# An attention-and-experts kernel: prologue, convolution stage and shared down projection rearranged

## The chip, the cores and the metric

The kernel runs on one core of a Trainium2 chip. The metric is device time in microseconds (us), the median of several executions. Engines are named as the profile names them: PE is TensorE (matmuls), DVE is VectorE, ACT is ScalarE, POOL is GpSimd, SP is SyncE, which here only issues transfers.

## The reference

`x` and `ctx_2048` are (8, 256, 512). Two blocks follow one another. Cut to what matters:

```python
# block 1: long convolution as attention, v = layernorm(x), x1 = x2 = ctx
kv  = v[:, h, :, None, :] * x2[:, h, None, :, :]        # 32 heads h of 8 rows: outer product over rows
y   = irfft(rfft(kv) * rfft(k[h]))[..., :L] + kv * bias  # causal convolution over L = 512
x   = x + einsum('bhijl,bhil->bhjl', y, x1)
# block 2: experts on layernorm(x)
scores = sigmoid(xf @ gate_w.T); top 2 of 8, weights normalised, times 2.5
shared = (silu(xf @ shared_wg.T) * (xf @ shared_wu.T)) @ shared_wd.T      # 704 hidden
routed = sum over the 2 picked experts of w * expert(xf)                  # 352 hidden each
x = x + shared + routed
```

## The kernel before, in words

The convolution is done as matmuls against Toeplitz blocks of the filter. Every f32 operand is split into a high and a low f16 part, and a product is three matmuls (high·high, high·low, low·high: `split_products`, lines 753 to 755). A head has 4 output blocks and 10 block pairs, so 30 matmuls of 128x512.

The 32 heads run in order, in four groups `g` of `HG` = 8. For head `s`, GpSimd makes the outer product `kv` (`outer`, L603, four instructions), ScalarE rounds it to the high part (`high_parts`, L1013) and reverses the filter (`turn_filter`, L1006), and the low part is a subtraction, on VectorE (`low_parts`, L1247) if `s` is in `DVE_LOWS` and on GpSimd (L628, four instructions) otherwise. TensorE convolves (`convolve`), VectorE multiplies each bank with the context (`products`, L1261) and sums (`total`, L1268). The buffers are a ring: `kv` has two, the parts have three, banks 0 to 3 hold a convolution, banks 4 and 5 the shared experts' gate and up, and banks 6 and 7 are taken in turn by all small work (`take`, `turn_bank`), in an order written out in `turn_order`: who takes a bank waits until the one two places before has been read.

Around the heads, in each engine's program by hand: before group `g` its rows are normalised (`value_moments`, `inverse_root`, `values`), transposed by TensorE (`prepare`, L775) and copied out (`turned`, L1045). The skip term takes `skip_product` (L1299), a matmul (`skip_sum`, L789) and `skip_term` (L1306, L1307) for each of four tiles. After the group the result is transposed back (`mix_out`) and added (`mixed`, L1415), its moments taken (`moments`, L1274), `feed_norm` and `feed_low` write its two parts, DMA transposes them (`turn_rows`), and while group `g` is convolved the rows of `g-1` go through `logits`, `scores`, `pick`, `ranks`, `pairs` (the row numbers in the experts' table), `gate_up` (six steps), `gated`, and one group later `down` and `add_shared`. The 704 hidden units are five tiles of 128 and one half tile of 64, which is tile 0. When the last group is done the experts' weights have been loaded (`expert`), and 39 tiles of 128 routed rows are computed in a loop to the end.

The prologue: SyncE loads the filters, the first rows `x_tok`, the constants and `ctx_hidden` (`cT`), in this order. The filters are split and stored to be read back repeated for every partition. The first rows are normalised as one piece, transposed through banks 6 and 7, copied by VectorE (`first_turned`, L1234), multiplied by GpSimd (`first_outer`, L619), rounded by ScalarE (L1018), and subtracted by VectorE (`first_low_parts`, L1241).

Of the kernel before, what the change touches and what calls it, by code (L numbers as in the profile page):

```python
# [50 lines left out]
DVE_LOWS = (0, 1, 5) + tuple(range(HG, H, 2))  # L51
# [3 lines left out]
def xattn_moe(nc, x, ctx, ctx_hidden, skip, krev, gate_w, shared_w, expert_w, consts, table0, zeros, out):  # L55
    split_filters = nc.dram_tensor("split_filters", [H, 2 * KREV], F16).ap()
    filters = bass.AP(split_filters.tensor, 0, [[2 * KREV, H], [1, P], [KREV, 2], [1, L]])
    x_rows = x.rearrange("b (g r) l -> g b r l", r=RG)
# [5 lines left out]
    with ExitStack() as stack:  # L64
# [138 lines left out]
        const_in = sem("const_in")  # L203
        small_in = sem("small_in")
        x_in = [sem(f"x_in{g}") for g in range(G)]
        ctx_in = [sem(f"ctx_in{g}") for g in range(G)]
        cT_in = [sem(f"cT_in{g}") for g in range(G)]
        filt_all_in = sem("filt_all_in")
# [103 lines left out]
        def turn_bank(name, g, k):  # L312

            n = sum(len(list(turns_of(*w))) for w in turn_order[:turn_order.index((name, g))])
            return bank[6 + (n + k) % 2]

# [29 lines left out]
        def shared_loads(i):  # L346

            return 2 if 0 < i < DOWN_AT else 1
# [37 lines left out]
        def _(sp):  # L386
            def load_filter(s):
                if s > 0:
                    sp.wait_ge(filt_ready, s)
# [19 lines left out]
            def load_shared(i):  # L409
                if i >= DOWN_AT:  # L410
# [35 lines left out]
            sp.dma_start(gate_raw[:], gate_w).then_inc(small_in, 16)  # L446
            sp.wait_ge(filt_stored, 16)
            load_filter(0)
            load_rows(ctx_tok, ctx_rows[0], ctx_in[0])
# [25 lines left out]
            for g in range(1, G):  # L475
# [12 lines left out]
                if g < G - 1:  # L488
# [8 lines left out]
                for h in range(5, HG + 2):  # L497
                    if s0 + h < H:
                        load_filter(s0 + h)

# [91 lines left out]
        def _(pool):  # L592
# [15 lines left out]
            def first_outer():  # L608

                v, c = heads(vT[0])[:, :, 0:NH], heads(cT[0])[:, :, 0:NH]  # L610
                pool.wait_ge(cT_in[0], 16)
                for q in range(Q):
                    pool.wait_ge(tokT_done, q + 1)
                    pairs_of = B // Q
                    to = by_tile(kv[0], q).rearrange("p a (b j i) -> p a b j i", i=NH, j=NH)
# [1057 lines left out]
```

## Time and profile before

| | us |
|---|---|
| median of 3 runs (758.6 to 763.07) | 761.96 |
| the profiled execution | 757.6 |
| its span | 755.8 |

The profile cuts the span in 40 slices and gives for each engine the tenths of busy time:

```profile
PE   2786976969989979999999998979899999999991
...
DVE  4799599767877668776778576784422221212210
...
POOL 2889988484783663874677404740132323223231
PEclk9999898979999998999999998989999999999996
```

PEclk is the TensorE clock that was granted, in tenths. A slice is 18.9 us: the heads end in slice 24, the rest is the experts. Idle time before a group of instructions is put down to what ended last.

### The profile page before, as it was taken

How to read it: one execution, taken by the hardware profiler on the slowest of the kernel's cores; microseconds unless marked ns; L12 is line 12 of the kernel's file. 1: busy time of each engine (PE TensorE's matmuls, PEld its weight loads, DVE VectorE, ACT ScalarE, POOL GpSimd, SP SyncE). 2: the span in 40 equal slices, each digit the busy share in tenths (PEclk: the TensorE clock that was granted, in tenths of full speed). 3: DMA queues.
4: the chain of work that ended last, by engine and by line, in shares of the span. 5: the costliest groups of instructions: out<-in, count | busy, mean ns of one | idle time of the engine just before them, and what ended most of it. 6: DMA issues, size and time to landing. Idle time of an engine off the chain costs nothing.

```text
span 755.8 us, 11521 instructions
## 1 busy us (share of the span) xinstructions
PE 663.5 (88%) x3441; PEld 329.3 (44%) x3442; DVE 438.5 (58%) x702; ACT 292.9 (39%) x362; POOL 387.2 (51%) x333
## 2 busy tenths in 40 slices
PE   2786976969989979999999998979899999999991
PEld 1332432434444434443444443425455555555550
DVE  4799599767877668776778576784422221212210
ACT  4336646534223443323243049543423232232320
POOL 2889988484783663874677404740132323223231
PEclk9999898979999998999999998989999999999996
DMA  7933222701333800313305079878897887878743
GB/s 204 275 97 97 84 69 68 162 9 29 126 79 74 183 15 19 113 38 70 84 15 200 14 270 262 297 195 262 162 125 127 138 128 129 131 125 140 129 62 42
DMA packets 130964, 91.56 MB, mean 121 GB/s; under 512 B 97664, under 2 KB 111488, under 8 KB 130368
## 3 DMA queue, kind: packets, MB, share of 16 engines
q1 hardware_dynamic: 121728, 72.44, 38.9%
q0 software_dynamic: 9200, 18.65, 14.0%
q8 instruction: 21, 0.34, 0.2%
q14 instruction: 15, 0.12, 0.1%
HBM read 44.35 MB, written 25.68 MB: 93 GB/s over the span
## 4 chain that ended last, share of the span: by engine, by line
PE 61%; DVE 14%; ACT 8%; POOL 7%; DMA 4%; issue 4%; SPq 1%; POOLq 0%; DVEq 0%; ACTq 0%
PE banks L753 20%; PE banks L754 19%; PE banks L755 19%; POOL arena L603 4%; PE banks L775 2%; DVE stats L1274 2%; DMA arena<-split_filters 2%; POOL arena L628 2%; DVE mixT L1268 1%; DVE arena L1261 1%; DMA out<-xf,ids 1%; ACT arena L1092 1%; DVE arena L1247 1%; DVE hm L1395 1%; DVE arena L1429 1%
## 5 line engine op out<-in xcount | busy, mean ns | idle before, releaser
L603 POOL TENSOR_TENSOR arena<-arena 128x512 f32<-128x512 f32 x124 | 136.1, 1130 | 67.0 <-DVE arena L1247 65.7
L716 POOL DMA_INDIRECT out<-xf,ids x39 | 61.2, 1569 | 185.8 <-DMA out<-xf,ids 142.5
L753 PE MATMUL banks<-arena 128*128 128x512 f16 x320 | 124.6, 389 | 21.0 <-DVE arena L1261 11.1
L754 PE MATMUL banks<-arena 128*128 128x512 f16 x320 | 124.2, 388 | 0.8 <-issue 0.8
L755 PE MATMUL banks<-arena 128*128 128x512 f16 x320 | 124.0, 387 | 0.0
L1261 DVE TENSOR_TENSOR arena<-banks,arena 128x512 f32<-128x512 f32 x128 | 81.3, 682 | 33.8 <-PE banks L755 28.6
L753 PE MATMUL banks<-arena,normed 128*128 x312 | 97.5, 313 | 0.9 <-DVE hm L1570 0.9
L754 PE MATMUL banks<-arena,normed 128*128 x312 | 97.5, 313 | 0.0
L755 PE MATMUL banks<-arena,normed 128*128 x312 | 97.5, 313 | 0.0
L1013 ACT ACTIVATE arena<-arena 128x2048 f16<-128x2048 f32 x31 | 59.1, 1906 | 87.5 <-POOL arena L603 87.5
L1568 DVE SCALAR_TENSOR_TENSOR hm<-banks,silu 128x256 f32<-128x256 f32 x39 | 16.5, 424 | 130.8 <-PE banks L755 120.0
L628 POOL TENSOR_TENSOR arena<-arena 128x512 f16<-128x512 f32 x68 | 78.8, 1193 | 7.6 <-ACT arena L1013 7.5
L1268 DVE TENSOR_REDUCE mixT<-arena 128x256 f32<-128x2048 f32 x32 | 73.1, 2285 | 1.0
L753 PE MATMUL banks<-xf,arena 128*128 128x512 f16 x176 | 69.2, 393 | 2.9 <-DVE hm L1395 2.8
L754 PE MATMUL banks<-xf,arena 128*128 128x512 f16 x176 | 69.0, 392 | 0.0
L755 PE MATMUL banks<-xf,arena 128*128 128x512 f16 x176 | 68.8, 391 | 0.0
L1006 ACT ACTIVATE arena<-arena 128x1024 f16<-128x1024 f16 x32 | 33.7, 1054 | 84.4 <-PE banks L755 71.3
L753 PEld LDWEIGHTS banks<-arena 128*128 128x128 f16 x320 | 31.9, 100 | 63.1 <-issue 20.4
L755 PEld LDWEIGHTS banks<-arena 128*128 128x128 f16 x320 | 31.9, 100 | 40.4 <-issue 4.4
L754 PEld LDWEIGHTS banks<-arena 128*128 128x128 f16 x320 | 31.9, 100 | 38.9 <-issue 4.8
L753 PE MATMUL banks<-arena,mixT 128*128 x117 | 44.4, 379 | 4.4 <-issue 2.7
L1185 ACT CAST x_tok<-hm 128x384 f16<-128x384 f32 x37 | 18.9, 511 | 73.5 <-DVE hm L1570 71.5
(168 smaller groups left out, 1095.6 us busy)
## 6 DMA issues: line engine op xcount, KB each, us to landing
arena<-split_filters SPq DMA_DIRECT2D x32, 256.0 KB
arena<-in_expert_w SPq DMA_DIRECT2D x12, 544.0 KB, 8.8
stages<-in_expert_w SPq DMA_DIRECT2D x10, 544.0 KB, 5.9
arena<-in_ctx_hidden SPq DMA_DIRECT2D x4, 1024.0 KB, 8.1
arena<-in_ctx SPq DMA_DIRECT2D x8, 512.0 KB, 6.5
x_tok<-in_x SPq DMA_DIRECT2D x6, 512.0 KB, 7.6
out<-x_tok SPq DMA_DIRECT2D x6, 512.0 KB, 6.0
x_tok<-in_expert_w SPq DMA_DIRECT2D x5, 544.0 KB
```

Of the source, the lines that this page charges most:

```text
L603: nc.gpsimd.tensor_tensor(kv[s % 2][:, lb * COLS:(lb + 1) * COLS].rearrange("p (b j i) -> p b j i", i=NH, j=NH), v[:, a, None, :].to_broad ...
L628: nc.gpsimd.tensor_tensor(kvl[s % SPLITS][:, c], kv[s % 2][:, c], kvh[s % SPLITS][:, c], ALU.subtract).then_inc(kvl_by_pool, 1)
L716: nc.gpsimd.indirect_dma_start(out=out, out_offset=bass.IndirectOffsetOnAxis(ap=ids[slot][:, 0:1], axis=0), in_=yg[slot], in_offset=None, ...
L753: nc.tensor.matmul(dst, wh, xh, start=(k == 0), stop=False)
L754: nc.tensor.matmul(dst, wh, xl, start=False, stop=False)
L755: last = nc.tensor.matmul(dst, wl, xh, start=False, stop=(k == n - 1))
L1006: nc.scalar.activation(filt[s % 2].rearrange("p (t l) -> p t l", t=2), back, ACT.Copy).then_inc(filt_ready, 1)
L1013: nc.scalar.activation(kvh[s % SPLITS], kv[s % 2], ACT.Copy).then_inc(kvh_ready, 1)
L1185: nc.scalar.copy(by_token[slot][:, 0:FK * P], hm[:, 0:FK * P]).then_inc(r_hh, 1)
L1261: nc.vector.tensor_tensor(prod[:, n * COLS:(n + 1) * COLS].rearrange("p (b j i) -> p b j i", i=NH, j=NH), bank[n].rearrange("p (b j i) -> ...
L1268: nc.vector.tensor_reduce(heads(mixT)[:, :, h * NH:(h + 1) * NH], prod.rearrange("p (a j i) -> p a j i", i=NH, j=NH), AX_X, ALU.add).then_ ...
L1568: nc.vector.scalar_tensor_tensor(out=hm[:, 0:whole], in0=bank[1][:, 0:whole], scalar=1 / WS, in1=silu[:, 0:whole], op0=ALU.mult, op1=ALU.mult)
```

## The change

The arithmetic is the same. The parts:

1. Prologue. `cT[0]` is loaded by a transfer that ScalarE issues first of all. The first rows come as two halves with a semaphore each, the constants as three (the small columns between the halves, then the identity, then the masks). The first filter is loaded directly as f32 and split by ScalarE and VectorE, no longer through the stored copy. Moments, root and shift go by halves; the four transposed tiles go to banks 4 to 7; `first_outer` is on VectorE and reads the banks; the copies to `vT` are on ScalarE, behind its rounding.
2. `DVE_LOWS`: heads 3, 7, 9 and 11 come to VectorE; 8, 10 and 12 go to GpSimd.
3. The skip term of group 1 moves from heads 4 to 7 into heads 11 and 12. The normalising of the next rows is split over two heads on TensorE and ScalarE. `rank` is behind `prep` in the turn order, `pairs` runs at the sixth head, and `inverse_root` behind the outer product.
4. After a group: the moments of tiles 0 and 1 are taken between the additions, `down(g-2, 0)` stands between the halves of `mix_out`, `add_shared` ahead of `feed_low`, and in group 1 `products` of head 9 ahead of `feed_low`. The context of group 2 is loaded later.
5. The half tile of `down`: the low part is written to rows 64 to 127 of `hTh` and the weights are doubled there, so one matmul gives two of the three terms: two matmuls in place of three.

```diff
-DVE_LOWS = (0, 1, 5) + tuple(range(HG, H, 2))
+DVE_LOWS = (0, 1, 3, 5, 7, 9, 11) + tuple(range(2 * HG - 2, H, 2))
...
-        turn_order = [("prep", 0), ("skip", 0), ("prep", 1), ("skip", 1)]
+        turn_order = [("skip", 0), ("prep", 1)]
         for g in range(1, G):
-            turn_order += [("out", g - 1), ("feed", g - 1), ("xf", g - 1), ("rank", g - 1)]
-            turn_order += [("prep", g + 1), ("skip", g + 1)] if g < G - 1 else []
+            turn_order += [("out", g - 1), ("feed", g - 1), ("xf", g - 1)]
+            turn_order += [("skip", 1)] if g == 1 else []
+            turn_order += [("prep", g + 1)] if g < G - 1 else []
+            turn_order += [("rank", g - 1)]
+            turn_order += [("skip", g + 1)] if g < G - 1 else []
...
             sp.dma_start(filt_all, krev).then_inc(filt_all_in, 16)
-            load_rows(x_tok[0], x_rows[0], x_in[0])
-            sp.dma_start(con[:], consts).then_inc(const_in, 16)
-            load_hidden(0)
+            for half in range(2):
+                for b2 in range(2):
+                    sp.dma_start(x_tok[0][b2 * RG:(b2 + 1) * RG, 2 * half:2 * half + 2, :],
+                                 x_rows[0].rearrange("(q t) r l -> t r q l", t=2)[b2][:, 2 * half:2 * half + 2, :]
+                                 ).then_inc(first_x_in[half], 16)
+                if half == 0:
+                    sp.dma_start(con[:, 4 * P:CONST_W], consts[:, 4 * P:CONST_W]).then_inc(small_const_in, 16)
+            sp.dma_start(con[:, 0:P], consts[:, 0:P]).then_inc(const_in, 16)
+            sp.dma_start(filt_raw.bitcast(F32), first_filter).then_inc(first_filt_in, 16)
+            sp.dma_start(con[:, P:4 * P], consts[:, P:4 * P]).then_inc(masks_in, 16)
...
+            act.dma_start(cT[0], ctx_hidden[0]).then_inc(cT_in[0], 16)
             act.wait_ge(filt_all_in, 16)
...
-            values(0)
-            turn_filter(0)
+            act.wait_ge(first_shift, 1)
+            layer_norm(x_tok[0], v_ready, range(0, 2))
+            first_filter_high()
+            act.wait_ge(first_shift, 2)
+            layer_norm(x_tok[0], v_ready, range(2, Q))
             first_high_parts()
+            first_turned()
             high_parts(1)
...
+            def first_outer(q):
+                dve.wait_ge(tokT_ready, q + 1)
+                dve.wait_ge(cT_in[0], 16)
+                pairs_of = B // Q
+                v = first_bank[q].rearrange("p (a b r) -> p a b r", a=LB, b=pairs_of)[:, :, :, 0:NH]
+                c = heads(cT[0])[:, :, 0:NH]
+                to = by_tile(kv[0], q).rearrange("p a (b j i) -> p a b j i", i=NH, j=NH)
+                shape = [P, LB, NH, NH]
+                for b in range(pairs_of):
+                    a = slice(pairs_of * q + b, None, B)
+                    last = nc.vector.tensor_tensor(to[:, :, b], v[:, :, b, None, :].to_broadcast(shape),
+                                                   c[:, a, :, None].to_broadcast(shape), ALU.mult)
+                last.then_inc(first_kv, 1)
...
+            first_moments(0)
+            first_moments(1)
+            first_shift_by(0)
+            first_shift_by(1)
+            first_filter_low()
+            first_outer(0)
+            first_outer(1)
+            first_low(0)
+            first_outer(2)
+            first_low(1)
+            first_outer(3)
+            first_low(2)
+            first_low(3)
...
+            def down_products(g, q, first=0, end=SM):
+                dst, c = down_bank(g, q), slice(q * P, (q + 1) * P)
+                for k in range(first, end):
+                    w = slice(k * L, (k + 1) * L)
+                    nc.tensor.matmul(dst, hTh[:, k, c], d_h[:, w], start=(k == 0), stop=False)
+                    if half_tile(k):
+                        last = nc.tensor.matmul(dst, hTh[0:HALF, k, c], d_l[0:HALF, w], start=False, stop=False)
+                    else:
+                        nc.tensor.matmul(dst, hTl[:, k, c], d_h[:, w], start=False, stop=False)
+                        last = nc.tensor.matmul(dst, hTh[:, k, c], d_l[:, w], start=False, stop=(k == SM - 1))
+                return last
...
             for g in range(1, G):
                 s0 = g * HG
                 convolve(s0)
-                mix_out(g - 1)
+                mix_out(g - 1, range(0, 2))
                 if g > 1:
                     if g == 2:
                         pe.wait_ge(shared_l, SH_PIECES)
-                    for q in range(Q):
+                    down(g - 2, 0)
+                mix_out(g - 1, range(2, Q))
+                if g > 1:
+                    for q in range(1, Q):
                         down(g - 2, q)
...
                 convolve(s0 + 3, range(LB - 1, LB) if g == 1 else range(LB))
+                if g == 1:
+                    skip_sum(1, 0)
+                    skip_sum(1, 1)
                 gate_up(g - 1, 1)
-                ranks(g - 1)
+                if g == G - 1:
+                    ranks(g - 1)
                 convolve(s0 + 4)
+                if g == 1:
+                    skip_sum(1, 2)
+                    skip_sum(1, 3)
+                gate_up(g - 1, 2)
                 if g < G - 1:
                     prepare(g + 1, range(0, 2))
-                gate_up(g - 1, 2)
+                convolve(s0 + 5)
                 if g < G - 1:
                     prepare(g + 1, range(2, Q))
-                for h in range(5, HG):
+                gate_up(g - 1, 3)
+                if g < G - 1:
+                    ranks(g - 1)
+                for h in range(6, HG):
...
             def mixed(g):
                 for q in range(Q):
-                    if g == G - 1 and q == 2:
-                        expert(0, 1)
+                    if q == 2:
+                        if g == G - 1:
+                            expert(0, 1)
+                        dve.wait_ge(x1_done, Q * g + q)
+                        tile_moments(x_tok[g % 3], range(0, 2))
...
                 if g == 1:
+                    products(s0 + 1, 1, g)
                     feed_low(0, range(0, 2))
-                    products(s0 + 1, 1, g)
+                    total(s0 + 1, 1)
                     feed_low(0, range(2, Q))
-                    total(s0 + 1, 1)
...
+                if g == 1:
+                    skip_product(1, 0)
+                    skip_product(1, 1)
                 pick(g - 1)
...
-                    if h == 4:
+                    if h == (6 if g < G - 1 else 4):
                         pairs(g - 1)
```

## Rows read from the trace of the kernel before

**Rows 1.** The page: busy time of each engine, and the chain that ended last by engine
```profile
PE 663.5 (88%) x3441; PEld 329.3 (44%) x3442; DVE 438.5 (58%) x702; ACT 292.9 (39%) x362; POOL 387.2 (51%) x333
...
PE 61%; DVE 14%; ACT 8%; POOL 7%; DMA 4%; issue 4%; SPq 1%; POOLq 0%; DVEq 0%; ACTq 0%
```

**Rows 2.** Windows by stage: length, busy of each engine, granted clock, DMA share, GB/s
```profile
0.00:23.57 23.57, 3.84 (x17) 3.05 (x18) 10.95 (x23) 9.06 (x12) 9.07 (x16) 1.00 0.84 210
23.57:105.91 82.34, 68.43 (x273) 29.95 (x274) 70.09 (x75) 41.63 (x39) 74.78 (x62) 0.94 0.42 117
105.91:215.04 109.13, 94.06 (x465) 43.95 (x466) 88.20 (x129) 49.80 (x52) 76.54 (x68) 0.92 0.31 82
215.04:331.45 116.41, 107.73 (x538) 49.93 (x537) 84.67 (x132) 43.64 (x47) 70.47 (x66) 0.97 0.33 80
331.45:437.51 106.06, 102.26 (x514) 46.28 (x513) 72.78 (x110) 32.36 (x35) 62.96 (x59) 0.98 0.26 70
437.51:525.65 88.14, 77.24 (x395) 34.39 (x393) 63.99 (x122) 49.61 (x60) 32.18 (x25) 0.92 0.84 262
525.65:755.83 230.18, 209.89 (x1245) 121.80 (x1245) 47.81 (x116) 66.74 (x118) 61.20 (x39) 0.97 0.76 122
```

**Rows 3.** Waits of TensorE up to 530 us: total, times, longest
```profile
PE banks L775 <- ACT normed L1029: 16.5, 3, 13.8
PE banks L753 <- DVE arena L1261: 11.1, 4, 6.2
PE banks L775 <- DVE next_row L1341: 9.9, 2, 5.1
...
PE banks L775 <- ACT arena L1045: 5.8, 1, 5.8
...
PE banks L775 <- DVE x_tok L1415: 2.7, 2, 2.2
PE banks L775 <- DVE arena L1415: 2.2, 1, 2.2
```

**Rows 4.** The chain that ended last: start, length, what
```profile
2.04 6.24 DMA x_tok<-in_x
...
15.80 6.06 POOL arena L619 x8
...
29.24 0.22 PE banks L754
...
445.05 2.48 DVE stats L1274 x4
```

**Rows 5.** Windows inside the first eleven microseconds, columns as in rows 2
```profile
3.00:8.00 5.00, 0.00 (x0) 0.00 (x0) 0.81 (x1) 1.10 (x2) 0.00 (x0) 1.00 1.05 244
8.00:11.00 3.00, 0.00 (x0) 0.00 (x0) 2.66 (x7) 0.00 (x0) 0.00 (x0) 1.00 1.01 401
```

**Rows 6.** Groups of GpSimd, 23.57 to 105.91 us: count, busy, mean ns, idle before
```profile
L603 POOL TENSOR_TENSOR arena<-arena 128x512 f32<-128x512 f32 x36 | 41.4, 1181 | 5.0 <-DVE arena L1247 4.5 <-POOL arena L628 0.2
L628 POOL TENSOR_TENSOR arena<-arena 128x512 f16<-128x512 f32 x20 | 24.3, 1245 | 0.0
```

**Rows 7.** Timeline of GpSimd, 96 to 106 us
```profile
100.88 2.13 POOL L658 TENSOR_TENSOR arena<-stages,arena 128x1024 f16<-128x1024 f32 x1
```

**Rows 8.** Groups of VectorE, 23.57 to 105.91 us
```profile
L1261 DVE TENSOR_TENSOR arena<-banks,arena 128x512 f32<-128x512 f32 x30 | 19.2, 681 | 11.7 <-PE banks L755 11.7
...
L1247 DVE TENSOR_TENSOR arena<-arena 128x2048 f16<-128x2048 f32 x3 | 9.2, 3050 | 0.0
L1299 DVE SCALAR_TENSOR_TENSOR hm<-arena,skip_col,normed 128x512 f32<-128x512 f32 x4 | 7.4, 1843 | 0.0
...
L1306 DVE TENSOR_TENSOR banks<-banks,arena 128x512 f32<-128x512 f32 x8 | 5.5, 688 | 0.0
```

**Rows 9.** Windows around two stalls, columns as in rows 2
```profile
278.40:288.50 10.10, 4.50 (x15) 2.33 (x16) 6.16 (x20) 5.57 (x9) 6.72 (x6) 0.66 0.01 2
338.90:346.50 7.60, 5.41 (x21) 2.25 (x21) 6.53 (x14) 1.06 (x1) 7.50 (x8) 0.78 0.12 35
```

More of the change, by code:

```diff
@@ L315, in turn_bank, with backward @@
             return bank[6 + (n + k) % 2]
+        first_bank = bank[4:4 + Q]
+        def backward(raw, parts):
+            return bass.AP(raw.tensor, raw.offset + L - 1, [raw.ap[0], [L, parts], [-1, L]])
         def toeplitz(s, part, d):
@@ L409, in load_shared @@
             def load_shared(i):
+                if i == DOWN_AT:
+                    sp.dma_start(shared_raw(i)[:, L:SH_PIECE], shared_w[:, L:SH_PIECE]).then_inc(shared_in[i], 16)
+                    for copy in range(2):
+                        sp.dma_start(shared_raw(i)[copy * HALF:(copy + 1) * HALF, 0:L], shared_w[0:HALF, 0:L]
+                                     ).then_inc(shared_in[i], 16)
+                    return
                 if i >= DOWN_AT:
@@ L857, in _ @@
             pe.wait_ge(const_in, 16)
-            prepare(0)
+            for q in range(Q):
+                pe.wait_ge(v_ready, q + 1)
+                transpose_tile(first_bank[q], lambda lb: normed[:, q, lb * P:(lb + 1) * P], tokT_ready)
             convolve(0)
+            pe.wait_ge(tokT_done, Q)
+            pe.wait_ge(masks_in, 16)
             skip_sum(0, 0)
@@ L866, in _ @@
                 convolve(s)
-            prepare(1)
+            prepare(1, range(0, 2))
             convolve(5)
-            skip_sum(1, 0)
-            skip_sum(1, 1)
-            convolve(6)
-            skip_sum(1, 2)
-            skip_sum(1, 3)
-            convolve(7)
+            prepare(1, range(2, Q))
+            for s in range(6, HG):
+                convolve(s)
             for g in range(1, G):
@@ L1025, in next_parts, with layer_norm @@
                     high_parts(s + 1)
-            def layer_norm(src, done):
-                for q in range(Q):
+            def layer_norm(src, done, tiles=range(Q)):
+                for q in tiles:
                     nc.scalar.activation(normed[:, q, :], src[:, q, :], ACT.Identity, bias=shift[:, q:q + 1],
@@ L1270, in total, with tile_moments, moments @@
                                         ).then_inc(mix_done, 1)
-            def moments(src):
-                link(*[nc.vector.bn_stats(stats[:, q, :], src[:, q, :]) for q in range(Q)])
+            def tile_moments(src, tiles):
+                link(*[nc.vector.bn_stats(stats[:, q, :], src[:, q, :]) for q in tiles])
+            def moments(src, tiles=range(Q)):
+                tile_moments(src, tiles)
                 link(*[nc.vector.bn_aggr(meanvar[:, q, :], stats[:, q, :]) for q in range(Q)])
@@ L1417, in mixed @@
                 dve.wait_ge(x1_done, Q * (g + 1))
[L1418 removed]
+                moments(x_tok[g % 3], range(2, Q))
             def mixed_shift(g):
[L1422 removed]
+                dve.wait_ge(rstd_ready, 2 * g + 2 if g < G - 1 else 2 * G - 1)
                 shift_by(shift_ready)
```

192 lines of the change are left out of this document (107 added, 85 removed).

## The prediction, on record before the change was run

> **What bounds the kernel now.** The page comes first [rows 1]: TensorE is busy for 88% of the span and makes up 61% of the chain that ended last. It is the bound on average, so what can be gained is its idle time, its time at the lower clock, and matmuls left out. The windows by stage [rows 2] say where these lie. The first seven lines are the prologue, group 0, groups 1, 2 and 3, the shared experts' last part with the weights' arrival, and the routed tiles. TensorE is idle for 19.7 us of the prologue, 13.9 of group 0, 15.1 of group 1, 8.7 of group 2, 3.8 of group 3. The routed tiles, 230 us, are full and untouched. In group 0 GpSimd is busy 74.8 of 82.3 us and VectorE 70.1: three engines are near their limit there, and a stall mended on one meets another. In group 1 VectorE has 88.2 of 109.1; in groups 2 and 3 TensorE alone is full.
>
> The waits of TensorE [rows 3] name the stalls: the first rows' normalising (13.8 us of 16.5), products of VectorE that come late (6.2 us in group 1, most of the rest at the end of group 0), `prepare` waiting for `rank_used` (next_row, 5.1 in group 2, the rest in group 1), `prepare` waiting for ScalarE's copies (5.8, group 0), and `mix_out`, whose third tile waits for the addition of the first (2.2 in each of groups 2 and 3).
>
> **Prologue.** Before, the chain [rows 4] has the rows landing at 8.3 us and `first_outer` on GpSimd, eight instructions in 6.06 us. The transfer engines are full from 3 us on [rows 5]: 244 GB/s while rows of 2 KB and the constants pass, 401 GB/s while the context passes with its larger packets. The context, 1.05 MB, takes 2.6 us of them. Now it goes ahead of the rows or beside them. The rows' last half then lands after 80 KB of filters, 1.05 MB of rows and the context: I start at 3 us with 0.1 MB moved, add 1.03 MB / 244 = 4.2 and 2.6, and get 9.8, with the landing 10.1 us; before it was 8.3. If the context didn't delay the rows it would be 7.5. The first half doesn't help by itself: its shift stands on VectorE behind the second half's moments.
>
> The Trainium skill ("DMA: Bandwidth & Descriptors", section "Issuing engines are not separate DMA queues") says that transfers from several issuing engines interleave on the same 16 engines and save only the issuing time. No row here has a transfer that ScalarE issued. By that rule the landing is 10.1, by separate paths 7.5, and the prologue's gain 2.1 or about 4.5 us.
>
> From landing to the first outer product it was 8.3 to 15.8, 7.5 us [rows 4]. Of these go half the moments (1.2 of 2.48 for four tiles [rows 4]), the root of the first half, about 1.1 as it now lies beside the second half's moments, and the copy before the product, 0.7 (a bank of 512, as L1261 [rows 8]). So VectorE starts at 10.1 + 4.5 = 14.6, or a little before that with the filter, and sets the pace. Its filter part, eight products of 256 elements and four quarter subtractions aren't in the trace in this form. A product is at least half of 0.68 [rows 8] and at most GpSimd's 6.06 / 8 = 0.76 [rows 4]; I take 0.4, since the form is L1261's. A quarter of a low part is 3.05 / 4 = 0.76 [rows 8]. With the filter's 0.7 that is 0.7 + 3.1 + 3.1 = 6.9, and the first convolution starts at 21.5, not 23.57 [rows 2]. The copies to `vT` now stand behind the rounding on ScalarE, so I put head 1's outer product at 22.9, 1 us later than before (15.80 + 6.06 [rows 4]); its chain, with 4 x 1.18 [rows 6] and a low part of up to 3.05 [rows 8] in it, ends about when TensorE is done with head 0 and two skip matmuls. If it doesn't, the gain at head 1 is nothing. I let head 1 start 2.1 earlier. Gain 2.1, bounds 0 (products at 0.76) and 4.5.
>
> **Group 0.** GpSimd's sum decides. It ends outer product 9 and the shared piece behind it at 103.0 [rows 7]. Two low parts leave it: eight instructions by 1.245 = 10.0 us [rows 6]. With the earlier start (I take 1.4 of the 2.1, because outer 5 still waits for VectorE's low part of head 3) that is 91.6. Low part 8 is now its own: 4.6, ending at 96.2, and head 8's last block, 12 matmuls of 0.217 [rows 4], ends at 98.8; before, head 8 ended at 105.9 + 30 x 0.217 = 112.4. VectorE gains two low parts (6.1) and loses group 1's skip term (4 products of 1.84 or less, 8 additions of 0.69 [rows 8], about 12), so it ends nearly when GpSimd does. I take off 1.2 for six outer products whose pieces may be slower than the mean of 1.18 [rows 6] while VectorE runs low parts beside them. Head 8 ends 12.5 us earlier, 10.4 of them group 0's. The 5.8 us wait is gone with it, since ScalarE's copies are asked for before `kv` runs out.
>
> **Group 1.** The wait for `next_row` (4.8 of the 9.9 [rows 3]) goes, and `products` of head 9 come 3 us sooner. But the skip term arrives: VectorE has 88.2 + 12 = 100, and waits some 5 us for ScalarE inside `gated`. That makes 105 of a stage that took 109.1. TensorE would need 94.1 + 3.4 for the skip matmuls, less what it loses at half clock (0.92 over 109.1 us is 17 us at half; I put the work in them at 9, so 4.6). So VectorE is the bound and the stage can't give more than about 4. And TensorE's program is in order: `skip_sum(1, 0)` and `(1, 2)` stand ahead of `gate_up`, while their products are queued behind `gated` and the moments. I expect three new waits of 3 to 5 us, at head 11 and twice at `skip_sum`. Gain 2.0, bounds -6 and 8.
>
> **Group 2.** 8.7 us of idle [rows 2] go, 2.2 of them `mix_out` and 5.1 `prepare` [rows 3], and with them the half clock behind it: 0.66 over 10.1 us [rows 9] is 6.8 us at half, of which TensorE worked 3.9 (from the end of the wait on), so 1.95. Four matmuls fewer give 0.9. Sum 11.5; I take 10.5, since `skip_sum` may wait as in group 1. VectorE has 84.7 of 116.4, cover enough for the new places of `pairs` and the moments.
>
> **Group 3.** 2.2 for `mix_out`; 0.78 over 7.6 us [rows 9] is 3.3 at half, 1.7 lost; 0.9 of matmuls. Sum 4.8, taken 4.6.
>
> **Tail.** Behind group 3 the chain goes through the moments of four tiles, 2.48 at 445.05 [rows 4]. Two are now taken while VectorE waits for the transposes: 0.9. `down(2, 0)` is 0.2 shorter on the same chain and `down(3)` 0.9. Gain 2.0. The weights are asked for when buffers come free, so they move along.
>
> **Sum.** 2.1 + 10.4 + 2.0 + 10.5 + 4.6 + 2.0 = 31.6 us. Against the profiled execution's own 757.6 that is 726.0. The median of the runs lies 4.4 above that execution and the lowest 1.0, so I put a median 2 above: 728.
>
> **Rivals.** (a) Group 1 gives everything back: VectorE is the bound there and in group 0's end, the new waits at `skip_sum` reach 6 us each and cost the clock as well. Group 1 loses 6, group 0 gives 8 only, and the prologue nothing: 728 + 8 + 2.4 + 2.1 = 740. For it speaks the row of group 1 [rows 2]; against it that half of TensorE's old waits there are named and removed. (b) TensorE's stalls close better than I walk through them: prologue 4.5, group 1 gives 8, group 2 all of its 11.5: 2.4 + 6 + 1 more than the sum, 718. (c) Slower. The clock stays at its lower level. Group 1 has a mean of 0.92 [rows 2], 17 us at half. If the waits of 3 to 5 us that follow each other from head 8 to 12 kept the clock low through that stretch, some 50 us of matmuls would run at half and cost 50: 728 + 50 = 778. It decides from 32 us of matmuls more at half upward. Against it: in group 0, with 13.9 us of idle, the mean is 0.94 and 10 us were at half [rows 2], not the whole stage. The Trainium skill ("TensorE: Matmul & The Clock Gate", section "What's actually happening") has the throttled state as the default, which activity lifts; by it more waits are more such stretches. (d) No change to speak of: the routed part doesn't start earlier, since weights or the table of rows set its start. Then 757. Against it: TensorE is busy 77 of 88 us in that stage, and the transfers there wait for kernel events.
>
> **Chances.** Forecast (720 to 736) 0.54, (a) 0.22, (b) 0.17, (c) 0.04, (d) 0.03. All but (c) and (d) are faster: 0.93, 0.03 within 0.5%, 0.04 slower. Half a per cent, 3.8 us, is what runs that spread over 4.5 us can tell. The range, 716 to 743, leaves out about the outer half of (b) and (c), (d) and a little of (a).
>
> **What would show it.** Prologue: `x_tok` landing near 10 us and the first convolution near 21.5; near 19 is the other price. Group 0: head 8 ends near 99 and GpSimd has no gap in it. Group 1: waits of L789 or L753 for L1299 and L1261, VectorE over 95% busy, head 16 starting near 201. Group 2: no wait for L1341 or L1415, clock 1.00, length 105 to 106. Group 3: 101.5. Three matmuls in four tiles' worth of `down` are two. I am wrong if head 8 isn't earlier by 10, if the waits at `skip_sum` reach 6 us, or if the granted clock falls below 0.9 in a stage.

## The result, and the profile after

The changed kernel takes 754.39 us (median of 9 runs, 750.37 to 758.23), the kernel before 758.93 (9 runs, 757.66 to 763.07) beside it: a ratio of 0.993, 95% interval 0.990 to 0.996. It is faster by 0.7%, about 4.5 us, where 31.6 were forecast; 754 lies outside the range of 716 to 743. Measured again later it was 752.3 against 759.7, 0.9905 (0.988 to 0.993).

The page of the changed kernel, the lines that answer to [rows 1]:

```profile
PE 662.5 (88%) x3425; PEld 327.5 (44%) x3426; DVE 438.8 (58%) x710; ACT 293.9 (39%) x366; POOL 390.2 (52%) x322
...
PE 34%; DVE 20%; POOL 18%; ACT 10%; DMA 7%; issue 7%; another core or an unknown queue 2%; SPq 1%; POOLq 0%; DVEq 0%; ACTq 0%
```

TensorE is as busy as before, but its part of the chain that ended last fell from 61% to 34%, and GpSimd's rose from 7% to 18%. The kernel has not lost its waits: they have changed their owner. The windows by stage, cut at the same events as [rows 2]:

```profile
0.00:21.36 21.36, 3.81 (x17) 3.18 (x19) 10.53 (x28) 9.49 (x15) 1.63 (x7) 1.00 0.89 219
21.36:94.64 73.28, 62.30 (x265) 27.34 (x265) 62.54 (x70) 40.78 (x41) 71.43 (x56) 0.98 0.49 135
94.64:207.19 112.55, 101.17 (x473) 45.30 (x474) 89.01 (x133) 49.78 (x53) 84.44 (x69) 0.92 0.30 78
207.19:324.62 117.43, 108.24 (x535) 49.28 (x534) 89.01 (x132) 43.52 (x48) 72.14 (x66) 0.97 0.35 81
324.62:432.51 107.89, 101.42 (x511) 46.13 (x509) 75.41 (x114) 34.16 (x36) 66.73 (x61) 0.98 0.28 68
432.51:519.26 86.75, 74.05 (x386) 33.97 (x385) 64.50 (x122) 49.48 (x60) 32.18 (x25) 0.96 0.83 254
519.26:752.60 233.34, 211.47 (x1245) 122.28 (x1245) 47.82 (x116) 66.65 (x118) 61.66 (x39) 0.96 0.79 126
```

Groups 2 and 3 (lines 4 and 5) are longer in this trace than before, 117.4 for 116.4 and 107.9 for 106.1, though two waits were taken out of the one and one out of the other. The change is ahead by 2.2 us at the first convolution, 7.0 at head 8's end, 7.9 at head 16, 6.8 at head 24, 5.0 at the end of the heads, and 3.2 at the end. (A second pair of traces, below, divides the gain otherwise among the stages.) TensorE's waits up to 530 us, for [rows 3]:

```profile
PE banks L799 <- ACT normed L1087: 14.0, 1, 14.0
PE banks L777 <- DVE hm L1504: 13.5, 4, 4.6
PE banks L777 <- issue: 8.7, 3, 3.7
PE banks L777 <- DVE arena L1366: 8.4, 8, 3.0
PE banks L813 <- DVE hm L1408: 5.7, 5, 3.1
PE banks L777 <- DMA mixT<-x_tok: 4.2, 1, 4.2
```

The waits for `next_row` (L1341), for ScalarE's copies (L1045) and for `mix_out`'s addition (L1415) are gone, as forecast. In their place stand 13.5 us for `hm`, the gated product that `gate_up` needs to reuse its bank, 5.7 at `skip_sum` (L813), and 4.2 for the first routed tile's transposed rows. None of the three is among [rows 3]. In the kernel before, the same view has 3.4 us for `hm` in four waits (longest 1.4) and 0.5 at `skip_sum`, and the first routed tile waited 2.7.

### The profile page after: what moved, and what is told of

Same layout as the page of the kernel before. It is cut to its first block, busy times and chain, and to the rows that moved or that the text cites. A ratio compares the mean times of both kernels' runs of the same rounds, so it can differ in the third digit from the quotient of the medians.

```text
span 752.6 us, 11505 instructions
## 1 busy us (share of the span) xinstructions
PE 662.5 (88%) x3425; PEld 327.5 (44%) x3426; DVE 438.8 (58%) x710; ACT 293.9 (39%) x366; POOL 390.2 (52%) x322
## 4 chain that ended last, share of the span: by engine, by line
PE 34%; DVE 20%; POOL 18%; ACT 10%; DMA 7%; issue 7%; another core or an unknown queue 2%; SPq 1%; POOLq 0%; DVEq 0%; ACTq 0%
PE banks L777 11%; PE banks L778 11%; PE banks L779 11%; POOL arena L635 9%; POOL arena L650 4%; DMA x_tok<-in_x 3%; DVE arena L1366 2%; DVE mixT L1373 2%; POOL pair_table L674 2%; DVE arena L1542 2%; POOL arena L680 2%; DVE hm L1504 2%; DVE stats L1379 1%; ACT arena L1149 1%
## 5 line engine op out<-in xcount | busy, mean ns | idle before, releaser
L635 POOL TENSOR_TENSOR arena<-arena 128x512 f32<-128x512 f32 x124 | 142.0, 1177 | 74.3 <-ACT arena L1102 36.8
L777 PE MATMUL banks<-arena 128*128 128x512 f16 x320 | 125.2, 391 | 21.4 <-DVE arena L1366 8.4
L778 PE MATMUL banks<-arena,normed 128*128 x312 | 97.7, 313 | 0.0
L779 PE MATMUL banks<-arena,normed 128*128 x312 | 97.7, 313 | 0.0
L1366 DVE TENSOR_TENSOR arena<-banks,arena 128x512 f32<-128x512 f32 x128 | 81.0, 683 | 25.1 <-PE banks L779 21.2
L777 PE MATMUL banks<-xf,arena 128*128 128x512 f16 x176 | 69.0, 392 | 13.5 <-DVE hm L1504 13.5
```

The source lines that it names most:

```text
L635: nc.gpsimd.tensor_tensor(kv[s % 2][:, lb * COLS:(lb + 1) * COLS].rearrange("p (b j i) -> p b j i", i=NH, j=NH), v[:, a, None, :].to_broad ...
L777: nc.tensor.matmul(dst, wh, xh, start=(k == 0), stop=False)
L778: nc.tensor.matmul(dst, wh, xl, start=False, stop=False)
L779: last = nc.tensor.matmul(dst, wl, xh, start=False, stop=(k == n - 1))
L1366: nc.vector.tensor_tensor(prod[:, n * COLS:(n + 1) * COLS].rearrange("p (b j i) -> p b j i", i=NH, j=NH), bank[n].rearrange("p (b j i) -> ...
```

## The experiments

The kernel before measured 759.1, 753.4, 759.7 and 761.5 in the four series, so ratios are to the kernel before of the same series, and milestones are read from the traces. First four, one edit each on the changed kernel.

**The moments of group 3's rows.** In group 2 VectorE stood before `gated` in a wait for rows that landed late. The chain there, changed kernel:

```profile
236.60 6.51 DMA out<-x_tok
...
243.78 12.27 DMA x_tok<-in_x
...
256.08 2.48 DVE stats L1379 x4
...
259.20 0.70 DVE hm L1504
```

The edit puts the moments back behind `pick`:

```diff
-                if 1 < g < G - 1:
-                    value_moments(g + 1)
                 gated(g - 1, 0)
...
-                    if h == 3 and g == 1:
+                    if h == 3 and g < G - 1:
                         value_moments(g + 1)
```

> The changed kernel with one edit undone: in group 2 the moments of the next rows are taken again behind gated and pick, not ahead of them. Theory A: the 5.4 us that VectorE waits for the rows' transfer stand in front of hm, TensorE waits 4.6 us for it and loses 2.6 more at the lower clock. Without it group 2 is 5 to 8 us shorter and the kernel 5 to 8 us faster than the changed one, near 748. Theory B: GpSimd's chain is late there too, the wait only changes its name: under 2 us.

753.07 us, 0.9911 (0.989 to 0.994). Head 20 starts at 265.8, not 268.2, but head 21 at 282.5 and head 24 at 324.6, both as before the edit. The first wait for `hm` in group 2 is 3.4 for 4.6 us: the moments were late, and what stands behind them nearly as late. Theory B.

**Low part 8.** It was given back to VectorE, with low parts 9 and 11 to GpSimd:

```diff
-DVE_LOWS = (0, 1, 3, 5, 7, 9, 11) + tuple(range(2 * HG - 2, H, 2))
+DVE_LOWS = (0, 1, 3, 5, 7) + tuple(range(HG, H, 2))
```

> The changed kernel with the low parts of heads 8, 10 and 12 on VectorE and 9, 11 on GpSimd, as before the change; heads 3 and 7 stay with VectorE. Theory A: head 8 waits for GpSimd (6.5 us for its low part in place of 4.5), so head 8 ends 3 to 5 us earlier than 105.5; what is left at head 16 is smaller, since VectorE is the limit in group 1. Theory B: GpSimd's speed, slowed by VectorE beside it, is the limit whoever has head 8: head 8 ends within 1 us of 105.5.

751.42, 0.9907 (0.988 to 0.993). Head 8 ends at 98.8, 6.8 earlier. That is the time the prediction gave before it took off 1.2, though it had GpSimd do this low part. Theory A, by more than it said. Yet head 10 starts at 115.5 (changed kernel 115.1), and head 16 at 206.7 (207.2). TensorE waits 6.2 us at `skip_sum(1, 0)` rather than 3.1. Group 1 takes up what group 0 gives here.

**The sending of pairs**, eight indirect transfers on GpSimd:

```diff
                     elif h == 0 and g >= 2:
-                        send_pairs()
                     elif g > 0 and h == 1:
                         inverse_root(2 * g)
+                        if g >= 2:
+                            send_pairs()
```

> The changed kernel with the eight indirect transfers of send_pairs moved on GpSimd from ahead of the second head's low part to behind its inverse root, where it idles 11 us. Theory A: in groups 2 and 3 TensorE's gains were eaten because those 10 us stand ahead of the outer product, the rounding and feed_norm: groups 2 and 3 get 2 to 4 us shorter each, with the wait for hm in group 3 (3.4 us) mostly gone. Theory B: feed_norm is late for VectorE's sake: no change beyond 1 us.

748.89, 0.9877 (0.986 to 0.990). Group 2 takes 114.3, not 117.4, and group 3 up to the end of its heads 101.2, not 102.9: Theory A by the lengths. The wait for `hm` in group 3 did not mostly go, though: it is 2.6 for 3.4. The heads end 4.5 us earlier in the trace, and the end 5.8. Against the first measurement of the changed kernel (0.993) this is clear of the noise, against its second (0.9905) only just not.

**The context from SyncE's queue**, behind the rows, not from ScalarE's at the start:

```diff
+            load_hidden(0)
...
-            act.dma_start(cT[0], ctx_hidden[0]).then_inc(cT_in[0], 16)
```

> The changed kernel with the first context loaded by SyncE behind the rows, as before the change, instead of by ScalarE first of all. Theory A: both share the transfer engines, so the rows land earlier (last half near 8.5 to 9 instead of 11.2 us), and the first convolution starts 1.5 to 2.5 us earlier. Theory B: the first product then waits for the context, which lands later, and the start is no earlier than 21.4.

753.9, 0.993 (0.991 to 0.995). The first convolution starts at 21.25, not 21.36. The chain's first long piece in the changed kernel:

```profile
4.03 7.16 DMA x_tok<-in_x
```

and with the context behind the rows:

```profile
5.71 8.64 DMA arena<-in_krev
```

The rows' last half now comes earlier (VectorE's second shift at 11.1, not 13.8 us), so the context did delay them by 2.7. But the first filter, which now stands behind the context in SyncE's queue, lands at 14.4 and holds the same start. Theory B by the time, with the filter in the context's place. The prediction's price of 10.1 for the landing (11.2 measured) was the right one of its two. The Trainium skill ("DMA: Bandwidth & Descriptors", section "Issuing engines are not separate DMA queues") says that transfers started by different engines interleave on the same 16 DMA engines; the 2.7 us of this run agree.

**Three edits at once**: low parts, moments and sending.

> The changed kernel with three edits at once: low parts 9 and 11 back on GpSimd, the moments of group 3's rows back behind the picking of experts, and the sending of pairs behind GpSimd's inverse root. Theory A, the stalls are separate: head 8 ends at 98.8, group 1 takes the gain back until head 16 (206.6), groups 2 and 3 keep 3 and 2 us of the later sending (heads' end 422), and what the moments give at head 20 (2 us) is kept, since GpSimd's chain no longer waits behind the transfers: 746 to 748. Theory B, the moments only move the wait: as with the later sending alone, 748.5 to 749.5.

745.13, 0.988 (0.984 to 0.993), and 745.0 in the next series, 0.981 (0.976 to 0.987). Theory A, and a little beyond its 746 to 748: the heads end at 420, not 422. It is the best full kernel here, 1.2 to 1.9% faster than the kernel before.

**The kernel before with only the sending moved.**

```diff
                     elif h == 0 and g >= 2:
-                        send_pairs()
                     elif g > 0 and h == 1:
                         inverse_root(2 * g)
+                        if g >= 2:
+                            send_pairs()
```

> The kernel before with only the sending of pairs (8 indirect transfers, about 10 us of GpSimd) put behind its inverse root in groups 2 and 3. Theory A: in the kernel before, the late chain GpSimd, ScalarE, VectorE is hidden under TensorE's own waits for next_row and mix_out, so the edit gives less than 1.5 us: 757.5 to 760, against 5 us in the changed kernel. Theory B: the late chain costs both kernels alike: 754 to 755, and then the changed order uncovered nothing.

753.72 against 753.4: 0.9996 (0.997 to 1.003), Theory A by the time. The trace said otherwise: group 3 took 96.7 us up to the end of its heads, not 101.1. So it was run again:

> The kernel before with only the sending of pairs behind the inverse root, measured again with more rounds. In its first trace the two waits for mix_out's addition (2.2 us each) shrank to 0.5 and group 3 took 96.7 us, not 101, yet the ratio was 0.9996. Theory A, the gain is real and the first measurement missed it in its spread: ratio 0.993 to 0.996. Theory B, the gain is given back in the tail or by the clock: ratio 0.998 to 1.001, with 2 us or more lost behind the heads' end.

754.23 against 761.5: 0.992 (0.989 to 0.995), and group 3 took 98.4 with TensorE's granted clock at 1.00. My Theory A of the first run, that the sending was hidden in the kernel before, does not hold there. The two intervals don't overlap. But the edited kernel took 754 us both times: it is the kernel before that moved, 753.4 in the one series and 761.5 in the other, and there is no trace of it from either. So the size stays between nothing and 1% by the times. By the traces the heads end at 425.9 and 429.7, where the two traces of the kernel before have 432.5 and 435.5. The waits for `mix_out`'s addition, which the change removed by a new order of TensorE's program, shrink from 2.2 to 0.5 us by this one move.

**Group 1 with less VectorE work**, on the three edits. Most of group 1's skip term is left out: only an eighth of `skip_product`'s columns is computed, and `skip_term` has no multiplication. This kernel's output lacks that term.

```diff
+                w = slice(0, L // 8 if g == 1 else L)
...
+                if g != 1:
                     link(nc.vector.tensor_tensor(t, t, ctx_tok[:, q, :], ALU.mult))
```

> The kernel with the three edits, with most of VectorE's share of group 1's skip term left out (an eighth of each product's columns, and the multiplication of skip_term not done for group 1; the output lacks it): about 4 x 1.5 and 4 x 0.7 = 9 us less VectorE work in group 1. Theory A, VectorE is group 1's bound: head 16 starts 6 to 9 us earlier than with the three edits alone, and the waits at skip_sum fall below 1 us. Theory B, the waits there are of order, not of load (GpSimd's or ScalarE's chain is next): head 16 is at most 3 us earlier.

740.79. VectorE's work from head 8's end to head 16 fell by 4.5 us (85.3 to 80.7), half of what was expected. Head 16 starts at 205.3, for 206.5 and 205.7 in the two traces with the full term, and the wait at `skip_sum(1, 0)` is still 5.6, for 7.0 and 6.1. Theory B: it isn't VectorE's load. Of the 5.3 us by which the end is earlier in the trace, 3.8 lie behind the heads, where nothing was changed; the second trace with the full term has 2.9 of them too. The timeline of VectorE and ScalarE at that wait, three edits:

```profile
131.68 1.91 ACT L1060 ACTIVATE arena<-arena 128x2048 f16<-128x2048 f32 x1 [2.49 <-POOL arena L635]
133.61 1.28 ACT L1122 ACT_TABLE_LOAD   x1
134.90 0.20 ACT L1122 ACTIVATE score<-banks 128x32 f32<-128x32 f32 x1
135.12 1.28 ACT L1128 ACT_TABLE_LOAD   x1
136.41 0.59 ACT L1128 ACTIVATE silu<-banks 64x512 f32<-64x512 f32 x1
```

```profile
137.04 0.69 DVE L1504 SCALAR_TENSOR_TENSOR hm<-banks,silu 64x512 f32<-64x512 f32 x1 [6.56 <-ACT silu L1128]
138.41 0.69 DVE L1509 TENSOR_TENSOR hTh<-hm,hTh 64x512 f16<-64x512 f32 x1 [0.68 <-ACT hTh L1134]
139.13 0.75 DVE L1408 SCALAR_TENSOR_TENSOR hm<-arena,skip_col,normed 128x512 f32<-128x512 f32 x1
```

Read backwards: `skip_sum` waits for a product of VectorE (L1408), which stands behind `gated`. That waited 6.56 us for the silu. The silu stood on ScalarE behind two table loads and a high part, and the high part waited for GpSimd's outer product. VectorE is 79% busy in this stage, in the changed kernel too (89.0 of 112.6), where the prediction looked for over 95%, and it is idle at the wait.

**Work put into that wait.** On the three edits, three blocks of head 12 (18 matmuls, 3.9 us) ahead of `skip_sum(1, 0)`:

```diff
                 if g == 1:
+                    convolve(s0 + 4, range(0, LB - 1))
                     skip_sum(1, 0)
                     skip_sum(1, 1)
```

> The kernel with the three edits, with the first three blocks of head 12 (18 matmuls, 3.9 us) put ahead of skip_sum(1, 0) on TensorE, where it waits 7.0 us for VectorE's product behind gated. Theory A, the place of skip_sum is what costs group 1: head 13 starts 3 to 4 us earlier and head 16 keeps it (203), the end by as much. Theory B, the chain over GpSimd's outer product, ScalarE's high part and silu sets group 1's pace: TensorE waits for kv at head 13 or 14 instead, and head 16 is at most 1.5 us earlier.

745.08, beside 745.0 for its base in the same series. The first wait shrinks from 6.1 to 2.4 us, and one of 5.5 us opens at `skip_sum(1, 2)`, not at `kv` as Theory B said; head 13 starts at 164.7 (163.7), head 16 at 206.8 (205.7). Otherwise Theory B: group 1's pace does not come from the place of this TensorE work, and the chain over GpSimd, ScalarE and VectorE is what the timelines show at the wait.

Its base, and the two kernels themselves, were profiled again beside it.

> The kernel with the three edits once more, as the base for the next run: ratio 0.984 to 0.993, head 16 at 206.5, heads' end at 420.

> The changed kernel profiled once more. Ratio to the kernel before 0.990 to 0.996 as in the first measurement; waits of 2.6 to 4.6 us before the second products of group 1 and 2 and at the silu of group 3 at the same places.

> The kernel before, profiled once more on the chip of this series. Theory A, chips differ in their clock and transfers: its stages are each shorter or longer than in the first profile by up to 3 us in sum, with the same waits at the same places (next_row 5.1, mix_out 2.2). Theory B, the waits themselves vary from one execution to the next: the waits for mix_out's addition come and go, and a stage difference of 2 us between two kernels proves little.

The base came out as expected. The changed kernel had a span of 753.5, with its waits for `hm` and at `skip_sum` up to the heads' end the same within 0.8 us. The kernel before took 760.3 in one run, span 758.5, with the waits of [rows 3] at their places within 1.1. Its head 8 ended 2.7 us later. So single stages move by up to 3 us between executions, and a stage difference of 1 us proves nothing by itself.

The pair of second traces changes the account by stage. The change is ahead by 2.3 us at the first convolution, 8.5 at head 8's end, 7.7 at head 16, 10.8 at head 24, 9.5 at the end of the heads and 5.0 at the end. Group 2 is 3.2 us shorter there (118.9 to 115.7), not 1.0 longer, and the part behind the heads is 4.4 longer, not 1.8.

**GpSimd's outer product beside VectorE's low part.** In groups 2 and 3 of the changed kernel GpSimd needs 6.2 us for the outer product ahead of the silu. The edit, on the three, takes the low part from beside it:

```diff
-                low_parts(s0 + 4)
+                if g == 1:
+                    low_parts(s0 + 4)
...
                 gated(g - 1, 0)
+                if g > 1:
+                    low_parts(s0 + 4)
```

> The kernel with the three edits (745.1), with VectorE's low part of head s0 + 4 behind gated(g - 1, 0) in groups 2 and 3, where VectorE waits some 6 us for the silu. Theory A, the low part beside it is what makes GpSimd's outer product take 6.2 us rather than 4.1: that outer product takes 4.2, the high part and the silu come 2 us earlier, the waits for hm in groups 2 and 3 (2.8 and 2.5) fall below 1, and the end is 3 to 5 us earlier. Theory B, the low part slows the next piece of GpSimd's just as much, or picking and the moments come late instead: within 1 us of 745.

749.46, 0.986 (0.984 to 0.988), no faster than its base (0.981 and 0.988). Its timeline of GpSimd and then of VectorE in group 2:

```profile
242.67 4.14 POOL L635 TENSOR_TENSOR arena<-arena 128x512 f32<-128x512 f32 x4
258.09 4.13 POOL L635 TENSOR_TENSOR arena<-arena 128x512 f32<-128x512 f32 x4 [11.28 <-DVE arena L1352]
```

```profile
255.72 2.29 DVE L1352 TENSOR_TENSOR arena<-arena 128x2048 f16<-128x2048 f32 x1
...
259.22 2.03 DVE L1435 TENSOR_TENSOR onehot<-con,topf 128x32 f32<-128x32 f32 x2
261.28 0.99 DVE L1438 TENSOR_TENSOR picked<-onehot 128x32 f16<-128x32 f32 x1
```

Theory A holds for the mechanism: 4.14 us, and the wait for `hm` falls from 2.8 to 1.9 in group 2 and from 2.5 to 0.5 in group 3. It fails for the time: GpSimd waits 11.3 us for the late low part before its next outer product, the collision moves to the picking of experts (2.03 and 0.99 us, for 0.42 and 0.19 elsewhere), and TensorE waits 6.4 us at head 20.

**The low parts shared out as before**, on the changed kernel: `DVE_LOWS = (0, 1, 5) + tuple(range(HG, H, 2))`.

> The changed kernel with the low parts shared out as in the kernel before (VectorE 0, 1, 5 and every second from 8 on; two more for GpSimd in group 0). Theory A, GpSimd's sum sets group 0 and its gain is kept: head 8 ends at 108 to 110 and head 16 starts 3 us later than in the changed kernel (210), the end at 757. Theory B, group 1's waits at skip_sum take up any lateness of group 0, as they took up the 6.8 us of the low part of head 8: head 16 within 1.5 us of 207.2 and the end within 2 us of the changed kernel.

755.76, 0.993 (0.991 to 0.996). Head 8 ends at 104.5, 1.1 *earlier* than in the changed kernel, and head 16 starts at 210.9, 3.7 later. By head 16 and the end this is Theory A; the lateness was not taken up. Head 8 is no test of GpSimd's load here, because its own low part went to VectorE in the same edit. The run with low part 8 on VectorE differs from this one in heads 3 and 7 alone. Against it the two low parts more on GpSimd make head 8 end 5.7 us later (104.5 for 98.8) and head 16 start 4.2 later (210.9 for 206.7). The two low parts are 10 us of GpSimd by the prediction's sum. They come out as 5.7 at head 8, since without them TensorE goes from head 7 to head 8 with no wait and is the limit itself. And group 1 passes on most of a lateness that comes from GpSimd.

**The tail.** On the three edits, the last expert's weights are asked for behind the first tile's transposed rows:

```diff
                 turn_hidden(t, t % 2)
                 if t == 0:
+                    load_expert(E - 1)
```

> The kernel with the three edits, with the last expert's weights asked for behind the first routed tile's transposing transfer, not ahead of it. Theory A, the first hidden tile waits for a full set of transfer engines: its transfer takes 3 us rather than 7.5, the wait of 4.2 us at the first down product goes, and the end comes 2 to 4 us earlier. Theory B, what the first tile gains is lost at the next ones or at the weights' rounding: within 1 us.

747.84, 0.992 (0.989 to 0.995), beside 745.13. The first tile's second product starts 14.7 us behind its first, not 18.0, and then TensorE waits 3.95 us for the same kind of transfer at 521.6. Theory A is out for the time. The intervals overlap, so that the kernel is slower by 2.7 us isn't shown. That the weights take the transfer engines from one tile or from the next fits the two waits; no run shows it by itself.

## Why the prediction was wrong

Of its three signs of being wrong one came: head 8 is earlier by 7.0 us, not by 10. The waits at `skip_sum` stayed at 3.1 and below, and the lowest granted clock of a stage was 0.92.

**Prologue, 2.1: right, in part by luck.** 2.2 measured, and the first convolution at 21.4, for 21.5. But the landing was at 11.2 rather than 10.1, and VectorE started at 15.1, not 14.6. Its filter part, products and subtractions then took 6.1 us, not 6.9, and the two misses cancel.

**Group 0, 10.4: half of it came.** Head 8 ended 7.0 earlier, not 12.5, at 105.5. The step "Two low parts leave it: eight instructions by 1.245" held. (GpSimd gets to low part 8 at 93.4, for 91.6.) The next, low part 8 "is now its own: 4.6, ending at 96.2", is mis-sized. The timeline of GpSimd, changed kernel:

```profile
93.38 6.54 POOL L650 TENSOR_TENSOR arena<-arena 128x512 f16<-128x512 f32 x4
```

It took 6.54 and ended at 99.9. One of its four pieces alone took 3.21 us, from 94.5 to 97.7, while VectorE's low part of the next head ran beside it. TensorE stood before head 8 for 3.7 us, and from 97.8 on did 27 of its 30 matmuls at a mean granted clock of 0.78 (98.0 to 105.6 us). So the last block began at 102.8 and not as soon as the low part was done: about 3 us of the lateness lie there, and the prediction had no term for them. I had a row for the cause: VectorE's three low parts took 3.05 us each in group 0 [rows 8], where the run with the low part behind `gated` has one at 2.29. Both engines are slowed when they meet, and I allowed 1.2 us for it in six outer products and nothing in the low part.

**Group 1, 2.0: 0.85 came, inside the bounds, and the reason was wrong.** "VectorE has 88.2 + 12 = 100" became 89.0 of 112.6 us. From head 8's end to head 16 VectorE's work went from 82.4 to 85.0, not up by 12: there is one low part less in the stretch, and `skip_product` takes 1.3 us rather than the 1.84 of [rows 8]. "So VectorE is the bound" fell with the run that took its work away. A wait of 3.1 at `skip_sum` came as forecast, but from the chain described above. The runs with low part 8 on VectorE and with head 12 ahead of `skip_sum` show that group 1 swallows time brought to TensorE there. The run with the low parts of before shows that it does not swallow a later GpSimd.

**Group 2, 10.5: the step that failed.** The stage is 1.0 us longer in the first pair of traces and 3.2 shorter in the second. The step subtracted TensorE's waits and the half clock behind them, with "VectorE has 84.7 of 116.4, cover enough". The waits did go, and others came: TensorE waited 8.7 us in group 2 before, and now waits 9.2, of them 6.2 for `hm` and 1.9 at `skip_sum`, with the stage's granted clock at 0.97 both times. A busy share is no cover. The question was how soon the next thing would be needed. In group 3, where moments play no part, both traces show it. ScalarE before:

```profile
376.34 1.91 ACT L1013 ACTIVATE arena<-arena 128x2048 f16<-128x2048 f32 x1 [1.78 <-POOL arena L603]
378.27 1.28 ACT L1065 ACT_TABLE_LOAD   x1
379.57 0.20 ACT L1065 ACTIVATE score<-banks 128x32 f32<-128x32 f32 x1
379.78 1.28 ACT L1071 ACT_TABLE_LOAD   x1
381.07 0.59 ACT L1071 ACTIVATE silu<-banks 64x512 f32<-64x512 f32 x1
```

and after:

```profile
370.06 1.91 ACT L1060 ACTIVATE arena<-arena 128x2048 f16<-128x2048 f32 x1 [6.45 <-POOL arena L635]
371.99 1.28 ACT L1122 ACT_TABLE_LOAD   x1
373.29 0.20 ACT L1122 ACTIVATE score<-banks 128x32 f32<-128x32 f32 x1
373.50 1.28 ACT L1128 ACT_TABLE_LOAD   x1
374.80 0.59 ACT L1128 ACTIVATE silu<-banks 64x512 f32<-64x512 f32 x1
```

Head 24 starts at 331.45 and 324.62. From there `hm` is done after 50.9 us before (382.39) and after 51.5 now (376.11). TensorE asked for its bank after 52.1 us before (383.51), 1.1 us after it was free. Now it asks after 48.1, and waits 3.4:

```profile
376.17 0.39 PE L777 MATMUL banks<-xf,arena 128*128 128x512 f16 x1 [3.44 <-DVE hm L1504]
```

The slack was 1.1 us and the gain forecast for group 3 was 4.6; with this producer unchanged only the first 1.1 could be had there. In group 2 `hm` was done 49.6 us after head 16's start before, 0.8 ahead of need, and 52.7 after. Of the 3.1, 1.2 are the late moments by the run that moved them. The rest fits the outer product of 6.2 us: in the kernel before VectorE's low part started at 258.3, just as that outer product had ended after 4.1 us, and now it starts inside it. So a wait of 4.6 us opened (255.3 to 260.0), and behind it TensorE was back at half clock for a while, though it had no pause in those 6 us (clock in the last column but two):

```profile
260.00:266.00 6.00, 6.00 (x17) 2.19 (x18) 5.26 (x16) 3.30 (x3) 5.92 (x6) 0.57 0.22 44
```

The half clock that I had counted as won came back with the new wait.

**Group 3, 4.6: the same step.** -1.8 measured (-1.4 in the second pair, up to the end of the heads). At the matmul shown the changed kernel is still 0.5 us ahead within the stage. The other 2.3 are lost behind it: TensorE waits 1.9 us for `picked` at 381.5, and its granted clock is 0.88 from 384 to 398, where the kernel before had 1.00 from 390 to 402. The second trace has no such wait, so this part is not the same in each execution.

**Tail, 2.0: not had.** It is 1.8 longer (325.1 us from the heads' end for 323.3), and 4.4 in the second pair. The wait at the first routed tile's second product is 4.2 us against 2.7 before, with a granted clock of 0.97 in the 60 us from 519.3 on, and 1.00 in those from 525.7 on before. That the weights' transfers reach it at another moment is a guess. Traces of edited kernels whose program behind the heads is the changed kernel's have 320.2 to 325.0 us for this part.

**The rivals.** Rival (a), group 1 gives everything back, did not happen: the lead was 7.0 us at head 8's end and 7.9 at head 16. It describes only what happened to the further 6.8 us that the run with low part 8 on VectorE brought, and its 740 left groups 2 and 3 whole. Rival (d), the end doesn't move, came nearest by its number, 757, but not by its reason: the routed part did start 6.9 us earlier. No rival said that TensorE comes to need the GpSimd chain's result about 1 us into the time that its old waits gave it. With group 2 and 3 at zero for 15.1, group 0 at 4.8 for 10.4 and the tail at zero, the sum is 9, still more than the 3.2 that came.

**What stays open.** The size of the later sending in the kernel before, and why that kernel took 753.4 us in one series (above); why the tail's first waits differ from one kernel to the next by 2 us; why group 2's length moves by 1.7 to 2.5 us between two traces of one kernel; and whether the chain of group 1 can be shortened, since no run tried to shorten ScalarE's part of it.

## What to carry to other kernels

Before subtracting a wait, find the next event due on the same engine and the time at which its producer is done, both counted from the start of the stage: the difference is all that the mend can give, and here it was about 1 us under waits of 2 to 5. A stage in which several engines are 70 to 90% busy may be set by a loop through all of them; work shifted between engines, or into a wait, then returns as another wait. Put work that nobody waits for (here eight indirect transfers) behind the work that the loop waits for: that one move brought the heads' end forward by 3.0 and 4.5 us against the two traces of the changed kernel, and by about 6 in the kernel before, where the whole change brought 5.0 and 9.5.

## What the runs showed of the hardware

In these traces a GpSimd operation and a VectorE operation that both read two inputs from SBUF do not run beside each other. In the changed kernel, VectorE beside the outer product:

```profile
246.44 10.27 POOL L635 TENSOR_TENSOR arena<-arena 128x512 f32<-128x512 f32 x8
248.02 2.65 DVE L1352 TENSOR_TENSOR arena<-arena 128x2048 f16<-128x2048 f32 x1
```

Eight pieces of 1.04 us would be 8.3; they take 10.3, 2 us more, about the length of the low part. One piece alone has the 2 us, 3.11 from 248.5 on; the low part, which started inside the piece before it, took 2.65 for 2.28. Without it four take 4.14 (the run with the low part behind `gated`). VectorE's products (L1366), which read one input from PSUM, cost GpSimd nothing: beside four of them, at 355.2 us, an outer product took 4.14 too. The Trainium skill ("SBUF — State Buffer", section "Who interferes with whom") says that a VectorE instruction with two SBUF inputs contends with a GpSimd instruction that reads SBUF, and that the one that comes second waits the other out; these rows agree, in both directions.

An indirect transfer occupies GpSimd for 0.96 us and 0.3 of issue, 1.27 in all, so eight hold up a low part by 10 us. Going to sigmoid and then to silu costs ScalarE two table loads of 1.28 us each, here on the path to `hm` in groups 1 and 3.
